# Earlier weight preparation, a last pair stored in two halves, and result operations moved behind the root in a conv, norm and table-FFN kernel

## The chip, the cores and the metric

The kernel runs on one core of a Trainium2 chip. The metric is the device time of one execution in microseconds, the median of several runs. The engines are named as the profile names them: PE is TensorE (PEld is its weight load), DVE is VectorE, ACT is ScalarE, POOL is GpSimd, SP is SyncE, whose queue here issues all transfers of x and of the result.

## The reference

The input x is 8 images of 256 channels by 64 by 64 pixels, f32.

```python
x = x + conv3x3_mean(ln_over_channels(x, eps=1e-6))   # 1/9 box, depthwise, zero padding
t = tokens(x)                                          # one token per pixel, 256 values
n = ln(t, eps=1e-5)
# four argmax nibbles of (n[16:80] > 0.5), two operator values and flags n[0:3] > 0.5
# build a sparse 80-wide row for two positions; three 80x80 layers with relu between (two weight sets);
# features 50 and 79 of the result give two rounded values 0..15 and a carry
out = n + 2*one_hot(lo) in 64..79 + 2*one_hot(hi) in 72..87 + carry in channel 80
x = image(t + out)
```

So per pixel: normalise over channels, blur, add, normalise again, and add to channels 64 to 87 what a small network says.

## The kernel before, in words

A pair of images lies in SBUF with its 2 x 64 rows on the 128 partitions, and for each partition 256 channels by 64 columns. There are 4 pairs, and a pair is worked in 8 chunks of 8 columns (CW), so there are 32 chunks. All engines run one software pipeline of 38 steps, written out in order for each engine (`run_steps`). In step t chunk t gets its first statistics, chunk t-1 is normalised (split into f16 high and low parts nhi and nlo), chunk t-2 is convolved, chunk t-3 is decoded and gets its final normalisation, chunks t-4 and t-5 are in the network, and chunk t-6 gets its result operations.

DVE's list in a step is the subject of most of the edit. `add_convolution(s)` (L570) adds the convolved pair of columns s from PSUM and waits for PE. `x_statistics` and `x1_statistics` (L552) are the variances. `finish(0..4)` are small operations: reciprocal of the root that ACT made, a Newton step, and in `finish(4)` the gains, shifts and the threshold `thr` (L456), whose semaphore `fin_ready` starts POOL (L659, L669) and the decoding. `put(0..7)` are the result operations of chunk t-6: `put(0)` waits for the transposed results of PE (`yt_done`, after L918) and runs L467 and L469, `put(4)` is the one-hot comparison L481, `put(5)` and `put(6)` (L488) and `put(7)` (L491) add into x and count `hotc`. `pick(0..2)` decode (L503, L505, L510, L513), and `normalise` (L542) makes the input of ACT's nhi (L816), which POOL's nlo (L650) and then PE's convolution (L864) need. POOL ends a step with the feature rows (L723), which PE transposes (L927) before it goes on to `convolve(1)`.

ACT applies the final normalisation to seven of the eight columns of a chunk (`columns`, L771), two, two and one of them in step t-3's groups s = 1, 2, 3 and the last two in the next step, and then counts `out_ready`. POOL does the eighth (L697, `out_p`).

The weights come through ACT's own queue (L756, 27 small transfers). `setup_parts` on DVE (L383 to L405) splits the first layer into three bf16 parts and runs at the start of step 2; PE's transposes of the weights (L840, L842) stand in its step 2 ahead of the first convolution; `setup_weights` on DVE (L409 to L415) copies them from PSUM in step 3.

SP stores channels in ranges. The range LATE is the one that the result operations write and waits for `hotc`; the ranges EARLY wait only for `out_ready` and `out_p`. Half a pair (32 columns) is stored at a time, so that one contiguous run in HBM is 128 bytes. The last pair is stored in four parts of 16 columns (LAST_PARTS), with runs of 64 bytes, one after the other in the queue: EARLY of a part, then its LATE, then the next part.

Of the kernel before, what the change touches and what calls it, by code (L numbers as in the profile page):

```python
# [9 lines left out]
ALU = mybir.AluOpType  # L10
# [13 lines left out]
GROUPS = CW // 2  # L24
HALVES = 2
HALF_W = W // HALVES
EARLY = ((0, C // 4), (C // 2, C))
LATE = (C // 4, C // 2)
RANGES = EARLY + (LATE,)


LAST_PARTS = (0, W // 4, W // 2, 3 * W // 4, W)


ALU_LO, ALU_HI, AX_LO, OP_COL, OUT_LO, OUT_HI, CARRY = 16, 32, 48, 65, 64, 72, 80
# [103 lines left out]
def build(nc, x_d, wa_d, ba_d, ws_d, bs_d, cst_d, out_d):  # L139
    with ExitStack() as ctx:  # L140
# [3 lines left out]
        def sem(name):  # L144
            return ctx.enter_context(nc.semaphore(name))
# [112 lines left out]
        y_read = sem("y_read")  # L258
        out_ready = sem("out_ready")
        out_p = sem("out_p")  # L260
        hotc = sem("hotc")

        def xview(parity):
# [9 lines left out]
        @block.sync  # L273
        def _(sp):
            def tile_part(parity, img, chans, cols):

                c0, c1 = chans
                return xbuf[img * H:(img + 1) * H, bass.ds(parity * (C * W) + c0 * W, (c1 - c0) * W)] \
                    .rearrange("p (c w) -> p c w", w=W)[:, :, cols[0]:cols[1]]

            def dram_part(ap, pair, img, chans, cols):
                return ap[bass.ds(pair * IMGS + img, 1), chans[0]:chans[1], :, cols[0]:cols[1]] \
                    .rearrange("b c h w -> (b h) c w")

            def load(pair, parity, chans, cols, loaded):
                for img in range(IMGS):
                    sp.dma_start(tile_part(parity, img, chans, cols), dram_part(x_d, pair, img, chans, cols)) \  # L287
                        .then_inc(loaded, 16)

            def store(pair, chans, cols, signal):  # L290
                for img in range(IMGS):
                    sp.dma_start(dram_part(out_d, pair, img, chans, cols),
                                 tile_part(pair % 2, img, chans, cols)).then_inc(signal, 16)

            sp.dma_start(cst[:, :], cst_d).then_inc(cst_loaded, 16)
            for pair in range(2):
                for h in range(HALVES):
                    if pair > 0:
                        sp.wait_ge(x_loaded[h], HALF_TILE * pair)
                    for chans in RANGES:  # L300
                        load(pair, pair, chans, (h * HALF_W, (h + 1) * HALF_W), x_loaded[h])

            def leave(pair, i, h):

                cols = (h * HALF_W, (h + 1) * HALF_W)
                store(pair, RANGES[i], cols, stored[h][i])

            def enter(pair, i, h):
                sp.wait_ge(stored[h][i], 16 * IMGS * (pair + 1))
                load(pair + 2, pair % 2, RANGES[i], (h * HALF_W, (h + 1) * HALF_W), x_loaded[h])  # L310

            def chunks_by(pair, h):

                return pair * CHUNKS + (h + 1) * (CHUNKS // HALVES)

            late = len(EARLY)
            with sp.Fori(0, PAIRS - 2) as pair:
                for h in range(HALVES):
                    sp.wait_ge(x_loaded[h], HALF_TILE * (pair + 2))
                for h in range(HALVES):  # L320
                    sp.wait_ge(out_ready, chunks_by(pair, h))
                    sp.wait_ge(out_p, chunks_by(pair, h))
                    for i in range(late):
                        leave(pair, i, h)
                    for i in range(late):
                        enter(pair, i, h)
                    sp.wait_ge(hotc, chunks_by(pair, h) * HOT_STEPS)
                    leave(pair, late, h)
                    enter(pair, late, h)
            pair = PAIRS - 2  # L330
            for h in range(HALVES):
                sp.wait_ge(out_ready, chunks_by(pair, h))
                sp.wait_ge(out_p, chunks_by(pair, h))
                for i in range(late):
                    leave(pair, i, h)
                sp.wait_ge(hotc, chunks_by(pair, h) * HOT_STEPS)
                leave(pair, late, h)
            pair = PAIRS - 1
            for cols in zip(LAST_PARTS, LAST_PARTS[1:]):
                chunks = pair * CHUNKS + cols[1] // CW  # L340
                sp.wait_ge(out_ready, chunks)
                sp.wait_ge(out_p, chunks)
                for chans in EARLY:
                    store(pair, chans, cols, last_stored)
                sp.wait_ge(hotc, chunks * HOT_STEPS)
                store(pair, LATE, cols, last_stored)
            for h in range(HALVES):
                for i in range(len(RANGES)):
                    sp.wait_ge(stored[h][i], 16 * IMGS * (PAIRS - 1))
            sp.wait_ge(last_stored, 16 * IMGS * len(RANGES) * (len(LAST_PARTS) - 1))  # L350

        @block.vector
        def _(v):
# [104 lines left out]
            def result(i, last, k):  # L458
# [14 lines left out]
                if i == 1:  # L473
                    v.tensor_reduce(ycar2, ycar, mybir.AxisListType.X, ALU.add).then_inc(y_read, 1)
                    hc.count(v.tensor_scalar(yr, yr, 1.0, float(NIB), ALU.max, ALU.min))
                elif i == 2:
                    hc.count(v.tensor_tensor(yr, yr, over(msk[:, k, :, :].unsqueeze(2), four), ALU.mult))
                elif i == 3:
                    hc.count(v.tensor_reduce(yrr, yr, mybir.AxisListType.X, ALU.add))
                elif i == 4:  # L480
                    hc.count(v.tensor_tensor(hot,  # L481
                                             over(cst[:, K_IOTA:K_IOTA + NIB].unsqueeze(1).unsqueeze(2), hot_shape),
                                             over(yrr.unsqueeze(3), hot_shape), ALU.is_equal))
                elif i in (5, 6):
                    at = OUT_LO if i == 5 else OUT_HI
                    v.wait_ge(out_ready, c + 1)
                    v.wait_ge(out_p, c + 1)
                    hc.count(v.scalar_tensor_tensor(cols[:, :, at:at + NIB], hot[:, :, i - 5, :], 2.0,  # L488
                                                    cols[:, :, at:at + NIB], ALU.mult, ALU.add))
                else:  # L490
                    hc.count(v.tensor_tensor(cols[:, :, CARRY], cols[:, :, CARRY], ycar2, ALU.add))  # L491
                    hc.end()
# [24 lines left out]
            def step(t, j, pair):  # L517
# [61 lines left out]
                    if tok:  # L579
                        decode(i, tok, (j - 1) % 4)  # L580

                if known(t) and t == 2:
                    setup_parts()
                if known(t) and t == 3:
                    setup_weights()
                if first:
                    half = {0: 0, CHUNKS // HALVES: 1}.get(j)
# [2 lines left out]
                add_convolution(0)  # L590
                x_statistics(0)
                wait_x1(0)
                put(0)
                x1_statistics(0)
                put(1)
                x_statistics(1)
                finish(0)
                put(2)
                finish(1)
                put(3)  # L600
                finish(2)
                put(4)
                finish(3)
                add_convolution(1)
                finish(4)
                if tok:
                    v.wait_ge(fin_ready, t)
                pick(0)
# [8 lines left out]
                normalise(CW - 2)  # L617
                wait_x1(2)
                pick(2)
                x1_statistics(2)  # L620
                x_statistics(2)
                put(5)
# [111 lines left out]
        def _(act):  # L734
# [25 lines left out]
            def step(t, j, pair):  # L760
# [5 lines left out]
                def columns(chunk, k, begin, end):  # L766

                    c, jc, par = chunk
                    for w in range(begin, end):
                        col = xview(par)[:, jc * CW + w, :]  # L770
                        ins = act.activation(col, col, ACT.Identity, bias=shift[:, k, w:w + 1],  # L771
                                             scale=gain[:, k, w:w + 1])
                    if end == CW - 1:
                        ins.then_inc(out_ready, 1)

                for s in range(GROUPS):
# [23 lines left out]
                        act.activation(s_sqrt[:, (j - 1) % 2, :], s_var[:, (j - 1) % 2, :],  # L800
                                       ACT.Sqrt).then_inc(sqrt_ready, 1)
                    if s == 0 and ffn:
                        columns(ffn, (j - 2) % 4, OUT_AT[GROUPS - 1], CW - 1)
                    if s == 0 and ffn:
                        c, jc, par = ffn
                        act.wait_ge(ft_done, c + 1)
# [16 lines left out]
                    if tok and s > 0:  # L823
                        if s == 1:
                            act.wait_ge(u_read, tok[0] + 1)
                            act.wait_ge(g_read, DV_STEPS * tok[0] + 1)
                        columns(tok, (j - 1) % 4, *OUT_AT[s - 1:s + 1])

            run_steps(act, step)

# [1 line left out]
        def _(pe):  # L832
# [35 lines left out]
            def step(t, j, pair):  # L868
# [1 line left out]
                ffn = chunk_at(t, j, pair, 4)  # L870
                back = chunk_at(t, j, pair, 5)
                last = chunk_at(t, j, pair, 6)
                if known(t) and t == 2:
                    setup_weights()
                if known(t) and t == 4:
                    pe.wait_ge(setup_v, SETUP_V)
                for s in range(GROUPS):
                    if conv:
# [96 lines left out]
```

## Time and profile before

| | |
|---|---|
| median of 3 runs | 617.44 us (616.48 to 617.96) |
| profiled execution | 618.25 us |
| its span in the profile | 616.5 us |
| DVE busy | 507.8 us (82%) |
| PE busy | 479.6 us (78%) |
| ACT busy | 468.7 us (76%) |
| POOL busy | 383.9 us (62%) |
| SP's transfer queue | 591696 packets, 67.30 MB |

The profiled execution took 1.75 us more than its span, for what lies around it. Busy shares are means over the whole span: the first 25 us are the load of the first half pair, then some steps fill the pipeline, then come some 26 full steps, and after about 545 us the pipeline drains.

### The profile page before, as it was taken

What the parts mean: (1) busy time and instruction counts of PE and PEld (TensorE: products, weight loads), DVE (VectorE), ACT (ScalarE), POOL (GpSimd) and SP (SyncE); (2) the same over time, 40 slices, a digit from 0 to 9 for tenths busy, and PEclk for the clock granted to TensorE, in tenths of its full rate; (3) what the DMA queues carried; (4) which work ended last, traced back from release to release, by engine and by line L of the source; (5) the groups of instructions that cost most, each with busy time, mean ns of one, the idle gap of its engine ahead of it and who ended that gap; (6) DMA issues with size and microseconds to landing.
All of it is one profiled execution on the core that took longest, in us unless ns stands there. A gap on an engine that the chain in (4) does not pass through costs nothing.

```text
span 616.5 us, 8862 instructions
## 1 busy us (share of the span) xinstructions
PE 479.6 (78%) x2294; PEld 201.1 (33%) x2294; DVE 507.8 (82%) x1476; ACT 468.7 (76%) x675; POOL 383.9 (62%) x676
## 2 busy tenths in 40 slices
PE   0035369999989988988899999988999999997750
PEld 0012123333333434333333333433333333433220
DVE  1378979999999999999999999999999999874130
ACT  0011569888888888899999888888888888998730
POOL 0044767777777777777777777777777777764000
PEclk9997779999999999999999999999999999998885
DMA  9999990099877995699559958960598099898998
GB/s 168 191 193 199 193 164 2 0 109 170 133 104 104 171 172 68 103 166 190 80 78 176 173 89 110 137 70 1 68 115 92 1 103 69 64 75 62 88 87 72
DMA packets 592746, 67.97 MB, mean 110 GB/s; under 512 B 592568, under 2 KB 592696, under 8 KB 592696
## 3 DMA queue, kind: packets, MB, share of 16 engines
q1 hardware_dynamic: 591696, 67.30, 88.5%
q8 instruction: 19, 0.31, 0.2%
q14 instruction: 31, 0.25, 0.1%
q10 hardware_dynamic: 1000, 0.11, 0.1%
HBM read 33.84 MB, written 33.55 MB: 109 GB/s over the span
## 4 chain that ended last, share of the span: by engine, by line
DVE 33%; PE 32%; POOL 12%; ACT 11%; issue 5%; SPq 3%; DMA 1%; DVEq 0%; POOLq 0%; ACTq 0%
PE ps L864 13%; PE ps L895 10%; POOL nlo L650 10%; DVE n L542 9%; DVE stat L552 7%; ACT nhi L816 5%; PE ps L918 4%; DVE g L505 4%; DVE xbuf L570 3%; ACT xbuf L771 3%; SPq L287 3%; PE ps L887 2%; DVE ps L481 2%; ACT h L791 1%; PE ps L900 1%
## 5 line engine op out<-in xcount | busy, mean ns | idle before, releaser
L771 ACT ACTIVATE xbuf<-xbuf,shift,gain 128x256 f32<-128x256 f32 x224 | 200.4, 944 | 0.0
L552 DVE BATCH_NORM_STATS2 stat<-xbuf 128x6 f32<-128x512 f32 x256 | 171.2, 685 | 22.0 <-DMA xbuf<-x 21.8
L650 POOL TENSOR_TENSOR nlo<-n,nhi 128x1024 f16<-128x1024 f32 x64 | 137.5, 2149 | 7.5 <-ACT nhi L816 7.4
L895 PE MATMUL ps<-h,w2m 128*128 128x512 f32 x256 | 134.3, 607 | 3.7 <-ACT h L791 2.4
L864 PE MATMUL ps<-nhi,band 128*128 128x512 f16 (+1 forms) x408 | 108.4, 380 | 25.1 <-POOL nlo L650 25.1
L669 POOL TENSOR_SCALAR n<-xbuf,stat,rns 128x256 f32<-128x256 f32 x64 | 94.2, 1478 | 41.4 <-DVE ps L456 41.0
L542 DVE SCALAR_TENSOR_TENSOR n<-xbuf,stat,ps 128x256 f32<-128x256 f32 x192 | 118.8, 663 | 0.1
L864 PE MATMUL ps<-nlo,band 128*128 128x512 f16 (+1 forms) x408 | 107.4, 377 | 0.0
L570 DVE TENSOR_TENSOR xbuf<-ps,xbuf 128x512 f32<-128x512 f32 x128 | 91.5, 715 | 15.6 <-PE ps L864 15.5
L816 ACT ACTIVATE nhi<-n 128x1024 f16<-128x1024 f32 x64 | 67.5, 1054 | 46.6 <-DVE n L542 46.6
L791 ACT ACTIVATE h<-ps,b2m 128x512 f32<-128x512 f32 x128 | 88.0, 687 | 11.4 <-PE ps L895 11.3
L783 ACT ACTIVATE h<-ps 128x512 f32<-128x512 f32 x128 | 75.7, 591 | 19.5 <-PE ps L887 19.5
L659 POOL TENSOR_TENSOR ut<-xbuf,stat 128x16 f32<-128x16 f32 x32 | 7.4, 230 | 123.8 <-DVE ps L456 123.8
L864 PEld LDWEIGHTS ps<-nhi,band 128*128 128x128 f16 x408 | 35.6, 100 | 110.9 <-issue 55.2
L887 PE MATMUL ps<-featT,w 128*128 128x512 bf16 x128 | 49.7, 388 | 28.4 <-ACT featT L808 26.4
L864 PEld LDWEIGHTS ps<-nlo,band 128*128 128x128 f16 x408 | 41.0, 100 | 45.5 <-issue 5.5
L895 PEld LDWEIGHTS ps<-h,w2m 128*128 128x128 f32 x256 | 45.6, 191 | 25.0 <-issue 17.6
L467 DVE SCALAR_TENSOR_TENSOR ps<-ps,msk 128x16 f32<-128x16 f32 x32 | 5.8, 183 | 47.9 <-PE ps L918 47.9
L723 POOL TENSOR_TENSOR feat<-val,msk 128x264 bf16<-128x264 bf16 x64 | 39.1, 635 | 0.2
L918 PEld LDWEIGHTS ps<-consts,ysb 128*128 128x128 f32 x256 | 33.5, 192 | 16.4 <-ACT ysb L821 9.0
L912 PE MATMUL ps<-h2r,w3r 128*128 128x512 f32 x64 | 36.0, 645 | 0.0
L900 PE MATMUL ps<-h,w2r 128*32 128x512 f32 x256 | 35.8, 633 | 0.0
(90 smaller groups left out, 560.0 us busy)
## 6 DMA issues: line engine op xcount, KB each, us to landing
xbuf<-x SPq DMA_DIRECT2D x32, 512.0 KB, 6.9
xbuf<-x SPq DMA_DIRECT2D x16, 1024.0 KB, 11.1
out<-xbuf SPq DMA_DIRECT2D x32, 512.0 KB, 7.4
out<-xbuf SPq DMA_DIRECT2D x12, 1024.0 KB, 12.6
out<-xbuf SPq DMA_DIRECT2D x16, 256.0 KB, 8.3
consts<-cst SPq DMA_DIRECT2D x1, 176.0 KB, 2.4
h<-ws ACTq DMA_DIRECT2D x4, 0.2 KB
b2r<-bs ACTq DMA_DIRECT2D x4, 0.1 KB
```

What stands on the lines that cost most here:

```text
L542: ins = v.scalar_tensor_tensor(n32[:, w // HALF, w % HALF, :], xview(par)[:, jc * CW + w, :], mean[:, k, w:w + 1], over(rn[:, w:w + 1], [P ...
L552: return v.bn_stats(stat[:, j % 4, at + 2 * s:at + 2 * s + 2, :].rearrange("p w n -> p (w n)"), xview(par)[:, w:w + 2, :].rearrange("p w c ...
L570: v.tensor_tensor(pair_cols, ps[:, B_CONV + s % 2, :].rearrange("p (w c) -> p c w", w=2), pair_cols, ALU.add).then_inc(x1_done, 1)
L650: pool.tensor_tensor(nlo[:, at:at + HALF, :], n32[:, h, :, :], nhi[:, at:at + HALF, :], ALU.subtract).then_inc(lo_ready, 1)
L669: pool.tensor_scalar(n32[:, h, HALF - 1, :], xview(par)[:, jc * CW + w, :], mean[:, k, w:w + 1], rns[:, j % 2, w:w + 1], ALU.subtract, ALU ...
L771: ins = act.activation(col, col, ACT.Identity, bias=shift[:, k, w:w + 1], scale=gain[:, k, w:w + 1])
L783: act.activation(h1[:, slot(i, jc), :], ps[:, B_L1, :], ACT.Relu).then_inc(h1_ready, 1)
L791: act.activation(h2[:, slot(i, jc), :], ps[:, B_L2, :], ACT.Relu, bias=b2m[:, 0:1]).then_inc(h2_ready, 1)
L816: act.activation(nhi[:, at:at + HALF, :], n32[:, s - 1, :, :], ACT.Copy).then_inc(hi_ready, 1)
L864: ins = pe.matmul(bank[:, i:i + k, :], band[:, :], src[:, at:at + k, :], start=n == 1, stop=n == 2 * len(pieces))
L887: pe.matmul(ps[:, B_L1, :], w1[:, i % 2, :], featT[:, jc % 2, i // 2, :], start=True, stop=True).then_inc(l1_done, 1)
L895: pe.matmul(ps[:, B_L2, :], w2m[:, :], h1[:, slot(i, jc), :], start=True, stop=True).then_inc(l2_done, 1)
```

## The change

The weights are prepared in step 0 on DVE and PE: parts, transposes and copies all stand before DVE's first wait for x. LATE shrinks from channels 64..127 to 64..95 and EARLY's second range grows to 96..255; this is so for all loads and stores. The last pair is stored in two parts of 32 columns. For the very last chunk ACT normalises columns 0 to 3 in one go, DVE columns 4 to 6 (a new `tensor_scalar`, with its own semaphore `out_v`), POOL the eighth as ever. In every step the statistics come before `finish(0)`, `put(0)` to `put(3)` each stand behind the `finish` of the same number, and `put(4)` behind `finish(4)`.

```diff
-EARLY = ((0, C // 4), (C // 2, C))
-LATE = (C // 4, C // 2)
+EARLY = ((0, C // 4), (3 * C // 8, C))
+LATE = (C // 4, 3 * C // 8)
-LAST_PARTS = (0, W // 4, W // 2, 3 * W // 4, W)
+LAST_PARTS = (0, W // 2, W)
 ...
                 sp.wait_ge(out_ready, chunks)
+                if chunks == NCHUNK:
+                    sp.wait_ge(out_v, 1)
 ...
-                if known(t) and t == 2:
+                if t == 0:
                     setup_parts()
-                if known(t) and t == 3:
                     setup_weights()
 ...
                 wait_x1(0)
-                put(0)
                 x1_statistics(0)
-                put(1)
                 x_statistics(1)
                 finish(0)
+                put(0)
+                finish(1)
+                put(1)
+                finish(2)
                 put(2)
-                finish(1)
+                finish(3)
                 put(3)
-                finish(2)
-                put(4)
-                finish(3)
                 add_convolution(1)
                 finish(4)
+                put(4)
                 if tok:
                     v.wait_ge(fin_ready, t)
                 pick(0)
 ...
                 pick(2)
+                if tok and tok[0] == NCHUNK - 1:
+                    c, jc, par = tok
+                    k = (j - 1) % 4
+                    v.wait_ge(u_read, c + 1)
+                    for w in range(HALF, CW - 1):
+                        col = xview(par)[:, jc * CW + w, :]
+                        ins = v.tensor_scalar(col, col, gain[:, k, w:w + 1], shift[:, k, w:w + 1], ALU.mult, ALU.add)
+                    ins.then_inc(out_v, 1)
 ...
                     if s == 0 and ffn:
-                        columns(ffn, (j - 2) % 4, OUT_AT[GROUPS - 1], CW - 1)
+                        if ffn[0] < NCHUNK - 1:
+                            columns(ffn, (j - 2) % 4, OUT_AT[GROUPS - 1], CW - 1)
 ...
-                        columns(tok, (j - 1) % 4, *OUT_AT[s - 1:s + 1])
+                        if tok[0] < NCHUNK - 1:
+                            columns(tok, (j - 1) % 4, *OUT_AT[s - 1:s + 1])
+                        elif s == 1:
+                            columns(tok, (j - 1) % 4, 0, HALF)
 ...
-                if known(t) and t == 2:
+                if t == 0:
                     setup_weights()
```

## Rows read from the trace of the kernel before

**Rows 1.** The page: span, and the busy share of the 16 DMA engines in 40 slices

```profile
span 616.5 us, 8862 instructions
DMA  9999990099877995699559958960598099898998
```

**Rows 2.** Timeline of the start: start us, us, engine, line, operation, [idle before, releaser]

```profile
25.55 2.47 DVE L552 BATCH_NORM_STATS2 stat<-xbuf 128x6 f32<-128x512 f32 x4 [21.82 <-DMA xbuf<-x]
...
34.04 4.21 POOL L650 TENSOR_TENSOR nlo<-n,nhi 128x1024 f16<-128x1024 f32 x2
...
36.11 2.23 DVE L386 COPY h<-h 128x2 f32<-128x2 f32 x2
...
40.54 0.09 DVE L404 MEMSET h<- 128x12 bf16 x2
...
41.80 1.27 PE L864 MATMUL ps<-nhi,band 128*128 128x512 f16 x3
...
44.24 0.72 DVE L570 TENSOR_TENSOR xbuf<-ps,xbuf 128x512 f32<-128x512 f32 x1 [3.61 <-PE ps L864]
...
57.78 1.49 PE L864 MATMUL ps<-nlo,band 128*128 128x512 f16 x3
...
59.68 0.73 DVE L570 TENSOR_TENSOR xbuf<-ps,xbuf 128x512 f32<-128x512 f32 x1
```

**Rows 3.** DMA queue of the weights: packets from 0 to 15 us, and all

```profile
q10 hardware_dynamic: 1000, 0.11, 5.4%
q10 hardware_dynamic: 1000, 0.11, 0.1%
```

**Rows 4.** Timeline of one full step, DVE, ACT and PE in order of time

```profile
291.50 0.17 DVE L456 TENSOR_TENSOR ps<-stat,ps 128x8 f32<-128x8 f32 x1
...
304.01 0.18 DVE L467 SCALAR_TENSOR_TENSOR ps<-ps,msk 128x16 f32<-128x16 f32 x1 [0.77 <-PE ps L918]
...
304.18 0.23 ACT L800 ACTIVATE s_sqrt<-s_var 128x16 f32<-128x16 f32 x1
...
304.39 0.62 PE L927 MATMUL ps<-identb,feat 128*128 128x128 bf16 x8 [0.52 <-POOL feat L723]
...
305.49 0.81 PE L864 MATMUL ps<-nlo,band 128*128 128x512 f16 x3
...
306.16 0.43 DVE L481 TENSOR_TENSOR ps<-consts,ps 128x256 f32<-128x256 f32 x1
...
306.58 0.71 DVE L570 TENSOR_TENSOR xbuf<-ps,xbuf 128x512 f32<-128x512 f32 x1
...
307.64 0.16 DVE L456 TENSOR_TENSOR ps<-stat,ps 128x8 f32<-128x8 f32 x1
307.83 0.18 DVE L503 TENSOR_TENSOR marks<-xbuf,ps 128x24 f32<-128x24 f32 x1
```

**Rows 5.** Timeline of the 33rd step, in which DVE waits for the second convolution

```profile
531.52 0.81 PE L864 MATMUL ps<-nlo,band 128*128 128x512 f16 x3
532.37 0.71 DVE L570 TENSOR_TENSOR xbuf<-ps,xbuf 128x512 f32<-128x512 f32 x1 [0.29 <-PE ps L864]
```

**Rows 6.** Timeline of the drain: ACT's columns of the last chunk, DVE's last operation

```profile
567.51 1.78 ACT L771 ACTIVATE xbuf<-xbuf,shift,gain 128x256 f32<-128x256 f32 x2
...
576.91 1.12 ACT L808 ACTIVATE featT<-ps 128x1024 bf16<-128x1024 bf16 x1
...
597.46 0.16 DVE L491 TENSOR_TENSOR xbuf<-xbuf,ps 128x8 f32<-128x8 f32 x1
```

**Rows 7.** Windows of the last store part: us, busy of PE, PEld, DVE, ACT, POOL, clock, DMA share, GB/s

```profile
577.80:601.00 23.20, 15.34 (x66) 5.40 (x66) 4.68 (x20) 8.47 (x14) 0.00 (x0) 0.81 1.17 88
```

**Rows 8.** DMA from 451.4 to 471 us, and the first store issued in it: KB, us to landing

```profile
q1 hardware_dynamic: 24617, 3.14, 140.9%
out<-xbuf SPq DMA_DIRECT2D x1, 512.0 KB, 4.9
```

**Rows 9.** Waits of SP's queue at the end: us in total, times, longest

```profile
SPq L350 <- DMA out<-xbuf: 5.1, 1, 5.1
```

More of the change, by code:

```diff
@@ L260, in build @@
         out_p = sem("out_p")
+        out_v = sem("out_v")
         hotc = sem("hotc")
@@ L486, in result @@
                     v.wait_ge(out_ready, c + 1)
+                    if c == NCHUNK - 1:
+                        v.wait_ge(out_v, 1)
                     v.wait_ge(out_p, c + 1)
@@ L772, in columns @@
                                              scale=gain[:, k, w:w + 1])
-                    if end == CW - 1:
+                    if end == CW - 1 or c == NCHUNK - 1:
                         ins.then_inc(out_ready, 1)
@@ L872, in step @@
                 last = chunk_at(t, j, pair, 6)
-                if known(t) and t == 2:
+                if t == 0:
                     setup_weights()
-                if known(t) and t == 4:
+                if t == 4:
                     pe.wait_ge(setup_v, SETUP_V)
```

## The prediction, as put on record

> **What bounds the kernel now.** I read the page first, then the timeline of its three stretches, since no mean describes them all. In the start nothing runs until 25.55 us, when DVE's first statistics stop waiting for x; DVE then waits again for PE, 3.61 us ahead of the eviction at 44.24 [rows 2]. In the full steps the chain goes round through all engines: from one threshold operation (L456, 291.50) to the next (307.64) it is 16.14 us, and DVE's only idle time in it is 0.77 us at `put(0)`, waiting for PE's transposed results [rows 4]. In the drain DVE's last operation ends at 597.62 [rows 6], but the span ends at 616.5 [rows 1]: the last 19 us are stores alone. They are late because the queue was still busy: the DMA slices are full there [rows 1], and the part before moved at only 88 GB/s in its 64-byte runs [rows 7]. So there are three places, each with its own limit.
>
> **Weights in step 0.** Before, the first convolution starts at 41.80, behind the weight work. Its input, the first of POOL's two low parts, is ready at half of 4.21 us after 34.04, so 36.15 [rows 2]. With about 0.14 us to hand it over, PE starts at 36.29; start to eviction is 44.24 - 41.80 = 2.44, so the eviction goes at 38.73 in place of 44.24: 5.5 us. The two statistics and the root that follow come after it in order, so the whole pipeline shifts. In step 3 the low-part matmuls of the first convolution end at 57.78 + 1.49 = 59.27, and the eviction goes at 59.68 because the weight copies lie between; with the 0.04 us that an eviction needs after its matmuls (531.52 + 0.81 = 532.33 against 532.37 [rows 5]) that is 0.37 more. Sum 5.9.
>
> What the move costs in its new place must fit before 25.55. All 1000 packets of ACT's queue have started by 15 us [rows 3]; landed they are by some 17, an estimate from the last starts and from a 512 KB store, which takes 4.9 us from issue to landing [rows 8] of which these small ones need only the end. The parts took 36.11 to 40.63 = 4.5 us, PE's transposes the time up to 41.80, 1.2 us [rows 2], and the five copies at most 1.2 (between 0.18 and 0.43 each, the small PSUM rows [rows 4]). 17 + 6.9 = 23.9, so it costs nothing under the load of x; the cover left is 1.6 us, and what exceeds it is paid one to one. Everything queued behind the wait for the weights on DVE (all statistics) would be late then; on PE and ACT nothing is. One of the copies, 36.11, takes 2.23 us with its neighbour and ends within 0.1 us of POOL's low part (34.04 + 4.21 = 38.25) [rows 2]. The Trainium skill (SBUF — State Buffer, Who interferes with whom) says that a DVE copy in a two-port mode and a GpSimd operation exclude each other for a whole instruction. The trace agrees with it, and by it, with POOL idle in step 0, the cover would be 3.7 instead of 1.6 us; the sum is the same.
>
> **Result operations later.** It looks as if 0.77 us a step, times some 26, would go. I don't take that. Take the wait away, and the next limit is the loop through POOL: L456 -> decode and three normalised columns -> nhi -> nlo -> POOL's list -> features -> L927 -> second convolution -> eviction -> `finish(4)` -> L456. PE's L927 waited for POOL's features, 0.52 us; the second convolution ends at 305.49 + 0.81 = 306.30, and DVE evicted it at 306.58 [rows 4], where 306.34 was possible. So that loop has 0.24 us to give: 15.90. Now `put(4)` stands between L456 and the decoding, in that very loop. It is 0.43 us long, and the next eviction follows it with one small operation between (306.16 to 306.58), so some 0.34 of it count [rows 4]; but between L456 at 307.64 and L503 at 307.83 DVE idles for the semaphore, 0.1 us of which it fills; I take 0.24 as what it adds. The loop comes to 15.90 + 0.24 = 16.14, as before: DVE's wait moves from `put(0)` to `add_convolution(1)`. Bounds: nothing added, -0.24 x 26 = -6.2 us; the whole 0.43 added, +0.19 x 26 = +4.9. The last two full steps waited at the eviction already, 0.29 [rows 5], and can only lose `put(4)`'s 0.24 each, +0.5; with a little gained in the first such step I book +0.2 for all of it. `finish(0)` now comes some 1.2 us earlier and needs ACT's root, which ends at 304.41 [rows 4]; DVE would arrive there within 0.1 us of that, and the chain from it to the eviction has more room than that.
>
> **The last chunk's columns.** Seven columns on ACT become four, in one go from 567.51. At 1.78 for two [rows 6] they end at about 571.0 instead of 577 (the copy that follows them started at 576.91 [rows 6]). DVE's three are a form that the trace doesn't show; between a 0.18 small operation and the 0.71 of an eviction twice as large [rows 4], so at most 2.1 us for three, or some 3 with a wait for POOL, which still ends before ACT's four. ACT's list after it is shorter by three columns, 2.7 us; ACT and PE hand each other tiles there and PE's own time fills part, so of 0 to 2.7 I take 0.9 off the end of the network.
>
> **Stores.** LATE's shrinking moves channels 96..127 to the stores that don't wait for results. In the middle no engine waits for these transfers, so it is free there. At the end: EARLY of the second half is 224 channels x 128 rows x 128 bytes = 3.67 MB. It starts at `out_ready`, 571.0 - 5.9 + 0.2 = 565.3 in new time. Rows 8 show what such a store costs: 3.14 MB in 128-byte runs between 451.4 and 471, so 19.3 us with its start; 7/6 of that is 22.5, to 587.8. The last result operation ends at 597.62 - 5.9 + 0.2 - 0.9 = 591.0. So the queue is empty then, and only LATE of a half is left, 0.52 MB: 4.9 us from issue for the same bytes [rows 8], 5.3 as it is two transfers. The wait on the last landing was 5.1 before [rows 9], much the same. To close I take 0.6, an estimate. 591.0 + 5.3 + 0.6 = 596.9.
>
> The Trainium skill (DMA: Bandwidth & Descriptors, Why small descriptors are slow) gives each packet a fixed 3 cycles beside one for each 32 bytes. By that a 128-byte run costs 7 where a 64-byte run costs 5, and the half would leave at 88 x 10/7 = 126 GB/s, the span ending at 601.7 as in rival 3; rows 8 show more, 3.14 MB / 19.3 us = 163 GB/s, and the sum goes by that.
>
> **Sum.** 616.5 - 596.9 = 19.6 us less. The profiled execution (618.25 with 1.75 around its span) lies 0.8 above the median 617.44, so the median should come to 596.9 + 1.75 - 0.8 = 597.8.
>
> **Rivals.** (1) The step loop gets shorter after all, because the wait that goes is not replaced: up to -6.2 us, 591.6. For it: DVE's only idle time goes; against: L927's wait for POOL. Chance 0.1. (2) `put(4)` in the loop costs its whole length, +4.9: 602.7. The gap of 0.19 before L503 speaks against. Chance 0.1. (3) The end stays bound by the queue: if the second half moves half way between 88 and 163 GB/s, at 126, EARLY takes 29.1 us from 566.3, to 595.4, and LATE 4.2, then 2.1 for landing and closing (4.9 less the 3.2 that 0.52 MB take at 163, with 0.4 to 0.6 to close): span 601.7, median 602.6. At the whole 88 of rows 7 it is 41.7 + 6.0 and the span 616, no change. Chance 0.13, of which 0.02 for no change. (4) The weights land late or their chain is slow, the cover of 1.6 is exceeded and most of the 5.9 goes: 603.5. Chance 0.06. (5) Slower than before: ACT's root. In step after step `finish(0)` to `finish(4)` and all of `put` now stand behind the wait for it, with only the statistics ahead. If the root came late enough for DVE to lose more than 0.75 us a step on top of 16.14, 26 steps would eat the 19.6; at 1 us a step it is 624. The root would have to be some 1.6 us later than its 304.41, and ACT runs in the same order as ever. Chance 0.03.
>
> **Numbers.** My forecast 597.8 has 0.58, with its own range of 594.5 to 600.5. The range of 592.5 to 603.5 takes in most of rivals 1 to 4. A measurement of this kernel tells some 0.2%, 1.2 us, from no change. Faster 0.95, within it 0.02, slower 0.03.
>
> **What would show it.** Right: first convolution on PE at about 36.3; L456 to L456 still about 16.1, with DVE idle ahead of L570 of the second convolution and none ahead of L467; ACT's L771 x4 once near 562; the last DVE operation near 591, and about 6 us behind it. Wrong: DVE's first statistics after 26; steps of 15.9 or 16.4; stores of the last half still moving when the results are done.

## The result, and the profile after

The changed kernel takes 596.5 us (median of 4 runs, 593.87 to 596.77), the kernel before 617.7 in the same session (616.48 to 618.1): ratio 0.965, 95% interval 0.962 to 0.968, so 3.5% faster, 1.3 us under the forecast of 597.8. The profiled execution is the fastest of the four, 593.87 with a span of 592.1; the other spans are 594.7 to 595.0. What I read from the profile is therefore some 2.6 us better than the median, and the section on the reasons says where.

The page of the kernel after (span; the busy share of the DMA engines in 40 slices; the chain that ended last, by engine):

```profile
span 592.1 us, 8823 instructions
...
DMA  9999990099945998299939994590209511990299
...
POOL 41%; DVE 23%; PE 17%; ACT 9%; issue 4%; SPq 3%; DMA 1%; POOLq 0%; ACTq 0%; DVEq 0%
```

A slice is 14.8 us. Where [rows 1] reads 8 or 9 from the 33rd slice to the end, four slices here, the 33rd, 34th, 37th and 38th, are almost empty (1, 1, 0 and 2). The last two still read 9; that the queue runs dry in the last one and then moves one short burst shows only in the windows further down. POOL has become the largest part of the chain (12% before).

The start, from the timeline (the columns are those of [rows 2]):

```profile
15.03 0.31 DVE L389 COPY h<-h 128x2 f32<-128x2 f32 x3 [11.25 <-DMA b<-bs]
...
17.54 0.09 DVE L407 MEMSET h<- 128x12 bf16 x2
...
17.94 1.06 PE L858 MATMUL ps<-consts,h 128*128 128x128 f32 x4
...
19.71 0.28 DVE L418 COPY w3r<-ps 128x128 f32<-128x128 f32 x1
...
25.75 2.47 DVE L557 BATCH_NORM_STATS2 stat<-xbuf 128x6 f32<-128x512 f32 x4 [5.77 <-DMA xbuf<-x]
...
34.26 4.19 POOL L662 TENSOR_TENSOR nlo<-n,nhi 128x1024 f16<-128x1024 f32 x2
...
36.43 1.25 PE L880 MATMUL ps<-nhi,band 128*128 128x512 f16 x3 [17.43 <-POOL nlo L662]
...
38.78 0.71 DVE L575 TENSOR_TENSOR xbuf<-ps,xbuf 128x512 f32<-128x512 f32 x1 [2.64 <-PE ps L880]
```

The weights are there at 15.03, all work on them is done at 19.99, and DVE then still waits 5.77 us for x. The first convolution starts at 36.43 (it was 41.80) and the first eviction at 38.78 (44.24).

One full step from the timeline, in order of time, and ahead of it the threshold operation (L459, before L456) of the 7th and, at the end, of the 31st step:

```profile
121.69 0.17 DVE L459 TENSOR_TENSOR ps<-stat,ps 128x8 f32<-128x8 f32 x1
...
295.48 0.62 PE L943 MATMUL ps<-identb,feat 128*128 128x128 bf16 x8 [0.50 <-POOL feat L735]
295.54 0.26 DVE L441 RECIPROCAL ps<-s_sqrt 128x16 f32<-128x16 f32 x1
295.71 0.12 DVE L470 SCALAR_TENSOR_TENSOR ps<-ps,msk 128x16 f32<-128x16 f32 x1
...
296.58 0.81 PE L880 MATMUL ps<-nlo,band 128*128 128x512 f16 x3
...
297.43 0.71 DVE L575 TENSOR_TENSOR xbuf<-ps,xbuf 128x512 f32<-128x512 f32 x1 [0.72 <-PE ps L880]
...
298.50 0.16 DVE L459 TENSOR_TENSOR ps<-stat,ps 128x8 f32<-128x8 f32 x1
...
298.57 0.42 DVE L484 TENSOR_TENSOR ps<-consts,ps 128x256 f32<-128x256 f32 x1
...
298.90 0.17 DVE L508 TENSOR_TENSOR marks<-xbuf,ps 128x24 f32<-128x24 f32 x1
...
507.59 0.17 DVE L459 TENSOR_TENSOR ps<-stat,ps 128x8 f32<-128x8 f32 x1
```

`put(0)` (L470) has no wait in front of it now; the wait stands at the eviction (L575), 0.72 us, and ends 0.04 us behind the second convolution (296.58 + 0.81 = 297.39). This is the wait that the prediction named. A step takes (507.59 - 121.69) / 24 = 16.08 us, against 16.14 in [rows 4] (16.16 as a mean of the same 24 steps of before).

The drain: DVE's new columns, ACT's four, and DVE's last operation from the timeline:

```profile
555.56 2.28 DVE L630 TENSOR_SCALAR xbuf<-xbuf,gain,shift 128x256 f32<-128x256 f32 x3
...
558.68 3.41 ACT L783 ACTIVATE xbuf<-xbuf,shift,gain 128x256 f32<-128x256 f32 x4
...
586.62 0.16 DVE L496 TENSOR_TENSOR xbuf<-xbuf,ps 128x8 f32<-128x8 f32 x1
```

The same stretch in windows (columns as in [rows 7]):

```profile
565.00:570.00 5.00, 3.63 (x25) 2.26 (x29) 2.34 (x10) 3.48 (x6) 0.00 (x0) 1.00 1.52 175
...
583.00:585.00 2.00, 0.97 (x8) 0.87 (x8) 0.71 (x5) 0.00 (x0) 0.00 (x0) 0.95 1.02 107
585.00:587.00 2.00, 0.00 (x0) 0.00 (x0) 1.60 (x6) 0.00 (x0) 0.00 (x0) 0.50 0.03 6
...
588.00:590.00 2.00, 0.00 (x0) 0.00 (x0) 0.00 (x0) 0.00 (x0) 0.00 (x0) 0.50 1.12 183
```

ACT's columns end at 562.09. EARLY of the second half then leaves at 175 GB/s, twice the 88 of [rows 7], and is over at about 584.3 (107 of 175 in the window from 583). Results are done at 586.78, 2.5 us later, and only LATE is left. From there to the end of the span it is 5.3 us.

### The profile page after: what moved, and what is told of

It reads as the page before. It is cut to its first block, busy times and chain, and to the rows that moved or that the text cites. A ratio compares the mean times of both kernels' runs of the same rounds, so it can differ in the third digit from the quotient of the medians.

```text
span 592.1 us, 8823 instructions
## 1 busy us (share of the span) xinstructions
PE 477.5 (81%) x2294; PEld 200.3 (34%) x2294; DVE 506.7 (86%) x1479; ACT 466.7 (79%) x672; POOL 384.6 (65%) x676
## 4 chain that ended last, share of the span: by engine, by line
POOL 41%; DVE 23%; PE 17%; ACT 9%; issue 4%; SPq 3%; DMA 1%; POOLq 0%; ACTq 0%; DVEq 0%
POOL nlo L662 21%; PE ps L880 9%; DVE n L547 8%; POOL feat L735 5%; ACT nhi L829 5%; DVE xbuf L575 4%; POOL xbuf L709 4%; DVE g L510 4%; SPq L288 3%; PE ps L943 3%; PE ps L911 2%; ACT xbuf L783 2%; DVE stat L557 2%; POOL nhit L718 1%; POOL val L706 1%
## 5 line engine op out<-in xcount | busy, mean ns | idle before, releaser
L783 ACT ACTIVATE xbuf<-xbuf,shift,gain 128x256 f32<-128x256 f32 x221 | 197.6, 944 | 0.0
L557 DVE BATCH_NORM_STATS2 stat<-xbuf 128x6 f32<-128x512 f32 x256 | 166.4, 683 | 5.8 <-DMA xbuf<-x 5.8
L575 DVE TENSOR_TENSOR xbuf<-ps,xbuf 128x512 f32<-128x512 f32 x128 | 91.7, 716 | 33.0 <-PE ps L880 33.0
L829 ACT ACTIVATE nhi<-n 128x1024 f16<-128x1024 f32 x64 | 67.5, 1054 | 38.2 <-DVE n L547 38.2
L916 PE MATMUL ps<-h,w2r 128*32 128x512 f32 x256 | 34.6, 613 | 0.0
L925 PE MATMUL ps<-h,w 128*32 128x512 f32 x256 | 34.1, 604 | 0.0
```

The lines of the kernel that those rows point to most:

```text
L557: return v.bn_stats(stat[:, j % 4, at + 2 * s:at + 2 * s + 2, :].rearrange("p w n -> p (w n)"), xview(par)[:, w:w + 2, :].rearrange("p w c ...
L575: v.tensor_tensor(pair_cols, ps[:, B_CONV + s % 2, :].rearrange("p (w c) -> p c w", w=2), pair_cols, ALU.add).then_inc(x1_done, 1)
L829: act.activation(nhi[:, at:at + HALF, :], n32[:, s - 1, :, :], ACT.Copy).then_inc(hi_ready, 1)
```

## The experiments

Each kernel was timed against the kernel before in the same session, whose median moved a little between sessions (617.05 to 618.43). So I compare ratios; 0.001 is 0.6 us.

### The three parts alone

**e1_weights** is the kernel before with only the weights in step 0:

```diff
-                if known(t) and t == 2:
+                if t == 0:
                     setup_parts()
-                if known(t) and t == 3:
                     setup_weights()
```

> The kernel before with the weight preparation in step 0 and nothing else. My theory, from the two traces: the whole pipeline moves up by what the first four steps show, 81.23 - 73.45 = 7.8 us at the threshold operation of step 4, of which the prediction had booked 5.9; so about 610 us (617.7 - 7.8). Rival: the additional 1.9 us of steps 3 and 4 come from the other parts of the change; then 611.8. Second rival: the first half load's end is the only thing that counts and the later steps wait for x; then less than 2 us.

612.24 us (610.83 to 614.75), ratio 0.9906 (0.9876 to 0.9935): 5.8 us less. The interval is 4.0 to 7.7 us, so the 5.9 of the prediction fits, and the 7.8 that was expected here, from the changed kernel's profile between its start and its sixth step, lies just outside. In e1's own profile the sixth threshold operation comes at 106.75, 6.69 us ahead of the kernel before, and both profiles have one long step at the start (17.29). The changed kernel's profile has none: some of the first steps may be 1.4 us longer or not from run to run, as the last experiments show.

**e2_stores** is the kernel before with only the ranges and the parts:

```diff
-EARLY = ((0, C // 4), (C // 2, C))
-LATE = (C // 4, C // 2)
+EARLY = ((0, C // 4), (3 * C // 8, C))
+LATE = (C // 4, 3 * C // 8)
-LAST_PARTS = (0, W // 4, W // 2, 3 * W // 4, W)
+LAST_PARTS = (0, W // 2, W)
```

> The kernel before with the new ranges and the last pair in two parts, nothing else. Theory: the second half's EARLY can start only when ACT's last two columns of the last chunk are done, at about 577.1, takes 22.5 us to 599.6, and LATE follows it, some 5 us with its landing: span about 605, median 606.3, a gain of 11.4. Rival: the queue is not the limit and the end follows the last result operation at 597.6 by 5.9 us: 604.7. Rival on the other side: starting the second half 10 us later than the third quarter did costs as much as the longer runs give: 617.

606.03 us (604.65 to 608.97), ratio 0.9791 (0.9756 to 0.9826): 12.1 us less (606.3 was expected), the largest part by far. 7.0 us lie between the last result operation (600.20) and the end of the span (607.2), against 5.3 in the changed kernel.

**e3_order** is the kernel before with only DVE's new order of `put` and `finish`:

```diff
                 wait_x1(0)
-                put(0)
                 x1_statistics(0)
-                put(1)
                 x_statistics(1)
                 finish(0)
+                put(0)
 ...
                 finish(4)
+                put(4)
```

> The kernel before with the new order of DVE's result operations, nothing else. Theory: the wait of 0.77 us a step at the first result operation reappears at the eviction of the second convolution, since the loop through POOL now holds the one-hot comparison; the step goes from 16.16 to about 16.07 us as in the trace of the changed kernel, so 26 x 0.09 = 2.4 us less: 615.3. Rival 1: the order is worth the whole wait, 20 us less. Rival 2: nothing, 617.7.

616.61 us (614.7 to 618.01, 12 runs), ratio 0.9973 (0.9955 to 0.9991): 1.5 us less (2.4 were expected), small but outside what the measurement leaves open. Its waits over the whole span (in total, times, longest):

```profile
DVE xbuf L570 <- PE ps L864: 34.7, 40, 3.4
...
DVE ps L467 <- PE ps L918: 23.7, 3, 11.3
```

In the kernel before, L467 waited 32 times, now 3 times (the drain), and the eviction 14 times, now 40. So the wait moved and did not go. The step is 16.08 us.

The three ratios multiply to 0.9906 x 0.9791 x 0.9973 = 0.967, and the whole change has 0.965, 1.4 us more. The split of the last chunk's columns is in the whole and in none of the three, and e5 below puts it at 2.7 us; the intervals of the three together are some 3 us wide to either side, so the parts add up as far as these runs can tell.

### What put(4) costs, and what bounds the step behind it

**e4_put4_early** is the changed kernel with `put(4)` out of the loop:

```diff
                 put(3)
+                put(4)
                 add_convolution(1)
                 finish(4)
-                put(4)
```

> The changed kernel with put(4) moved from behind finish(4) to ahead of add_convolution(1), where DVE waits 0.72 us for PE. Theory (the loop through POOL is the limit and put(4) stands in it with 0.21 us): the step goes from 16.07 to about 15.86, 27 x 0.21 = 5.7 us less, 596.5 - 5.7 = 590.8; DVE's wait at the eviction shrinks by about 0.5. Rival 1 (the step is limited by DVE's own list or by ACT's): no change, 596.5. Rival 2: the comparison now holds up the eviction, slower.

593.15 us (589.16 to 593.82), ratio 0.9576 (0.9545 to 0.9607). Its regular step is 15.91 us, so `put(4)` adds 16.08 - 15.91 = 0.17 a step. The median is 3.3 us (4.6 by the ratios) below the changed kernel's. 5.7 were expected, from 0.21 a step; 27 steps of 0.17 are 4.6. The profiled run, the slowest of the six, also has three long steps: 4, 5 and 10 take 17.33, 17.37 and 17.55 us. The step with 17.55, PE's timeline, behind the same instructions one step earlier:

```profile
153.41 0.62 PE L943 MATMUL ps<-identb,feat 128*128 128x128 bf16 x8 [0.50 <-POOL feat L735]
153.86 0.81 PE L880 MATMUL ps<-nhi,band 128*128 128x512 f16 x3
154.51 0.81 PE L880 MATMUL ps<-nlo,band 128*128 128x512 f16 x3
...
169.31 0.98 PE L943 MATMUL ps<-identb,feat 128*128 128x128 bf16 x8 [0.52 <-POOL feat L735]
170.09 1.49 PE L880 MATMUL ps<-nhi,band 128*128 128x512 f16 x3
171.37 1.49 PE L880 MATMUL ps<-nlo,band 128*128 128x512 f16 x3
```

And that kernel's windows, where the third number from the end is the granted clock:

```profile
166.00:170.00 4.00, 3.03 (x20) 2.14 (x20) 4.00 (x15) 4.00 (x8) 3.25 (x3) 0.93 0.47 80
170.00:174.00 4.00, 3.90 (x15) 1.56 (x18) 2.05 (x14) 2.44 (x4) 0.00 (x0) 0.65 0.47 72
```

The six convolution matmuls took 2.77 us from the first start to the last end where they take 1.46. The granted clock is 0.65 in the mean of the window, that is, partly at the lower of its two levels (1.2 GHz), after a stretch in which PE waited for POOL's features.

**e8_norm_first** goes on from e4: the first three normalised columns ahead of `pick(0)`, since nhi waits for them (ACT's L829: 0.42 us in the changed kernel, 0.26 in e4):

```diff
+                for w in range(HALF - 1):
+                    normalise(w)
                 if tok:
                     v.wait_ge(fin_ready, t)
                 pick(0)
-                for w in range(HALF - 1):
-                    normalise(w)
```

> The kernel e4_put4_early with pick(0) moved behind the first three normalised columns. Theory: ACT's nhi can start 0.9 us earlier after the threshold, POOL's own list then decides when the first nlo starts (0.2 us earlier), and the loop through POOL goes from 15.91 to about 15.7 a step, where ACT's list of 15.65 is the next limit: 27 x 0.2 = 5.4 us under e4, about 588. Rival 1: the step is limited by something else at 15.9, no change from e4, 593. Rival 2: PE's idle times grow and its clock falls more often, at 1.6 us each time; slower than 593.

585.11 us (583.0 to 587.24), ratio 0.945 (0.9423 to 0.9476). The step is 15.75 us (about 15.7 expected), and the kernel is 2.9 us faster than expected. Of the 8.0 us to e4 the steps give 27 x 0.16 = 4.3; in the profiles another 1.6 is e4's long tenth step, and the rest isn't explained. A piece of its chain of waits (start us, us, what):

```profile
297.27 0.23 POOL ut L671
297.50 3.03 POOL n L681 x2
300.53 0.20 POOL u L689
...
300.83 2.19 POOL nlo L662
```

Here POOL goes from the threshold to its low part without waiting for ACT. But POOL's loop isn't the only limit. DVE and PE at the end of the same step, from the timeline:

```profile
310.79 0.81 PE L880 MATMUL ps<-nlo,band 128*128 128x512 f16 x3
...
311.10 0.43 DVE L484 TENSOR_TENSOR ps<-consts,ps 128x256 f32<-128x256 f32 x1
...
311.63 0.71 DVE L575 TENSOR_TENSOR xbuf<-ps,xbuf 128x512 f32<-128x512 f32 x1
```

DVE's `put(4)` ends at 311.53, the convolution at 311.60, and the eviction starts at 311.63 with no wait in front of it. From 120 to 520 us DVE waits 1.2 us in all, where it waits 8.1 in e4 and 18.1 in the changed kernel. So DVE's own list and the loop through POOL are now about equally long, and a still shorter step needs less work in both; no run tests that.

### The columns and the stores of the end

**e5_no_split** is the changed kernel with all seven last columns on ACT, as before:

```diff
-                if tok and tok[0] == NCHUNK - 1:
 ...
-                        ins = v.tensor_scalar(col, col, gain[:, k, w:w + 1], shift[:, k, w:w + 1], ALU.mult, ALU.add)
-                    ins.then_inc(out_v, 1)
```

> The changed kernel, but ACT normalises all seven columns of the last chunk as in every other chunk. Theory: the second half's EARLY starts some 5.3 us later (about 567.5 instead of 562.2 in the trace's time) and its packets end at about 590 instead of 585, past the last result operation (586.8 + about 1 for ACT's longer list); LATE then queues behind them: about 2.5 to 3 us slower than the changed kernel, 599.5. Rival: the split only shortens ACT's list, 1 us: 597.6. Second rival: the queue was the limit already, then the whole 5.3: 602.

599.77 us (598.61 to 602.63), ratio 0.9694 (0.9656 to 0.9732): about 2.7 us more than the changed kernel (599.5 was expected). ACT's last column ends at 571.51, 9.4 us later than in the changed kernel. 2.7 us of that, as of the 5.1 us at the last operation (591.90 against 586.78), are two long steps at its start: 17.28 and 17.33, where the changed kernel's profile has 15.89 and 16.06. From the 34th threshold to the last operation it is 35.16 us here and 33.60 there, 1.6 more. Its windows behind the last operation:

```profile
592.00:594.00 2.00, 0.00 (x0) 0.00 (x0) 0.00 (x0) 0.00 (x0) 0.00 (x0) 0.67 1.39 148
594.00:596.00 2.00, 0.00 (x0) 0.00 (x0) 0.00 (x0) 0.00 (x0) 0.00 (x0) 0.50 0.99 153
596.00:598.00 2.00, 0.00 (x0) 0.00 (x0) 0.00 (x0) 0.00 (x0) 0.00 (x0) 0.50 0.74 114
```

The queue is still moving EARLY when the results are done, and the end is 599.1 - 591.9 = 7.2 us behind them, not 5.3. So 1.9 us of what the split of the columns brings is that the queue runs dry in time.

**e6_four_parts** is the changed kernel with four parts for the last pair again:

```diff
-LAST_PARTS = (0, W // 2, W)
+LAST_PARTS = (0, W // 4, W // 2, 3 * W // 4, W)
```

> The changed kernel with the last pair stored in four parts of 16 columns again (64-byte runs). Theory: from the 28th chunk's results at about 549 us on, 4.5 MB must leave at the 88 to 97 GB/s of such runs, 46 to 51 us, so the span ends near 600 to 603 and the median near 604.5, 8 us over the changed kernel. Rival: with the smaller LATE range and the earlier columns the four parts overlap as well with the drain as the two halves do: 597.

608.96 us (605.86 to 609.29), ratio 0.9841 (0.981 to 0.9872): 11.8 us more than the changed kernel, where 8 were expected. Its last result operation ends at 587.01, as in the changed kernel (586.78), but the span at 604.1: the queue carries 86 GB/s from 567 to 580 and 85 from 580 to 600, against 175.

**e7_late64** is the changed kernel with the channel ranges as before:

```diff
-EARLY = ((0, C // 4), (3 * C // 8, C))
-LATE = (C // 4, 3 * C // 8)
+EARLY = ((0, C // 4), (C // 2, C))
+LATE = (C // 4, C // 2)
```

> The changed kernel with LATE at channels 64 to 127 as before. Theory: what is left after the last result operation doubles from 0.52 to 1.05 MB, 4096 packets more at 1.35 to 1.7 a nanosecond, 2.4 to 3 us: 599.6. Rival: only the landing of the last packet counts, no change.

598.33 us (597.29 to 599.41), ratio 0.9673 (0.9641 to 0.9705): some 1.4 us more by the ratios, whose intervals overlap (599.6 was expected). In its profile the last operation ends at 587.2 and the span at 595.5, 8.3 us later where it was 5.3. So by the profile the smaller LATE is worth 3 us at the end, by the ratios half of it.

### Long steps and PE's clock

Are the long steps made by PE's clock? e5's kernel is the changed kernel up to the last chunk, so their profiles can be compared step by step. In the fourth step, ahead of the second convolution, the changed kernel (15.89 us) has

```profile
70.29 0.62 PE L943 MATMUL ps<-identb,feat 128*128 128x128 bf16 x8 [1.20 <-POOL feat L735]
70.74 0.81 PE L880 MATMUL ps<-nhi,band 128*128 128x512 f16 x3
```

and e5 (17.28 us)

```profile
70.70 1.03 PE L927 MATMUL ps<-identb,feat 128*128 128x128 bf16 x8 [2.37 <-POOL feat L723]
71.53 1.49 PE L864 MATMUL ps<-nhi,band 128*128 128x512 f16 x3
```

(L927 and L864 are the same instructions under e5's line numbers.) Over these transposes and the convolution the granted clock was 1.00 in the changed kernel (70.3 to 72.2 us) and 0.54 in e5 (70.7 to 74.1). If the clock makes the long steps, work for PE in its idle 0.50 us should prevent them. **e9_after_fill** is the changed kernel, **e10_put4_fill** e4 and **e11_norm_fill** e8, each with eight transposes that nobody reads, ahead of PE's wait for the features:

```diff
-                        pe.wait_ge(feat_ready, c + 1)
                         wait(pe, y_copied, c - 1)
+                        for b in range(CW):
+                            pe.transpose(ftp[:, b * P:(b + 1) * P], identb[:, :], identb[:, :])
+                        pe.wait_ge(feat_ready, c + 1)
```

> The changed kernel with eight transposes that nobody reads, put on PE ahead of its wait for the feature rows (line L943 and its wait), where PE idles 0.50 us in a step. They take 0.46 us each time, so they fit in the idle time and add at most 0.1 us to a step. If the long steps (17.2 to 17.6 us in place of 16.08) come from PE's granted clock, which fell ahead of L943 in them, PE has hardly any idle time left there, such steps become rarer or vanish, the slow step at the start goes too, and the median comes to the fastest run of the changed kernel or close: about 594, against 596.5. If they come from something else (a transfer, POOL), the fillers change nothing and the median stays at 596.5, or is some 1 to 2 us longer where they delay the transposes.

> The same eight fillers in the kernel with put(4) ahead of add_convolution(1), whose regular step is 15.91 us and in whose profile one step of the loop took 17.55 and two of the start 17.33 and 17.37, all three with L943 and the convolution at the lower clock level. Clock theory: steps of 15.91 throughout, no long ones, median near 590.5 against 593.15. Otherwise 593 or more, and long steps remain.

> The same eight fillers in the kernel that has the first three normalised columns ahead of pick(0), whose step is 15.75 us and whose median was 585.11. Its first steps were 16.99 and 17.24 long. Clock theory: those two come down to about 15.8 to 16, median near 583. Otherwise 585 or more.

| | without fillers | with | ratio without | ratio with | steps 4 and 5 without | with |
|---|---|---|---|---|---|---|
| changed kernel (e9) | 596.5 | 594.72 | 0.965 | 0.9627 | 15.89, 16.06 | 15.84, 15.86 |
| e4 (e10) | 593.15 | 590.09 | 0.9576 | 0.9554 | 17.33, 17.37 | 15.76, 16.77 |
| e8 (e11) | 585.11 | 583.35 | 0.945 | 0.9451 | 16.99, 17.24 | 15.56, 16.44 |

The tenth step, e4's long one, in e10's timeline:

```profile
165.90 0.61 PE L941 MATMUL ps<-identb 128*128 128x128 bf16 x8
166.55 0.62 PE L945 MATMUL ps<-identb,feat 128*128 128x128 bf16 x8
167.00 0.81 PE L880 MATMUL ps<-nhi,band 128*128 128x512 f16 x3
167.65 0.81 PE L880 MATMUL ps<-nlo,band 128*128 128x512 f16 x3
```

With fillers no profile has a step over 16.8 us, where e4 has three and e8 two over 16.9. That is one profile of each kernel, and it isn't proof: the profiles of the changed kernel, of e6 and of e7 have no such step without fillers either. e9's five runs lie within 0.9 us (594.18 to 595.04) where the changed kernel's four spread over 2.9, but e10's still spread over 1.9 and e11's over 3.1. The medians are lower by 1.8, 3.1 and 1.8, but the kernel before was also 0.7 to 1.4 us faster in that session: by the ratios it is 1.4, 1.4 and nothing, and the intervals overlap. So that a long step is one in which PE's transposes and the convolution behind them run at the lower clock is shown by the timelines; that the fillers prevent it is likely and not shown, and what they gain in the median isn't settled.

## Why the prediction was right, point by point

**Start, 5.9 us.** Right. PE's first convolution was forecast for about 36.3 and came at 36.43, the eviction for 38.73 and came at 38.78. The part alone measured 5.8. The threshold operation of the second step came 5.45 us earlier, that of the third 6.38: 5.9 were booked, so 0.5 more went in step 3 than the 0.37. By the sixth step the profiled run was 7.81 ahead. The 1.4 us between are the step of 17.29 us that the kernel before has at its start and this profile hasn't (15.89); that is this run, not the change.

**The cover.** Booked as 1.6 us, measured 5.77: the weights were there at 15.03 and not some 17, and the work took 5.0 us and not 6.9. The first copies took 0.31 us for three where one with its neighbour took 2.23 [rows 2], and POOL was idle. By the Trainium skill's rule (SBUF — State Buffer, Who interferes with whom), under which such a copy and a POOL operation exclude each other, a short copy was to be expected in step 0, and this trace agrees with it. Rival 4 needed the cover to be used up, and it was far from it.

**The order on DVE.** The mechanism is right: the wait went from `put(0)` to the eviction, and the loop through POOL is next to bound the step. The forecast for that loop without `put(4)` was 15.90, and e4 shows 15.91. The size of one term was off: `put(4)` was booked at 0.24 a step and measured 0.17 (16.08 - 15.91); the gap between the threshold and L508 grew from 0.19 [rows 4] to 0.40, 0.21. The step was to be 16.14 and is 16.08, and over the loop that is -1.5 (e3) or -1.9 (the profile: 7.81 ahead at the sixth step, 9.70 at the 34th) where I booked +0.2. Rivals 1 and 2 were the two ends of this term; the truth was a third of the way from my value towards the first. Rival 5 did not come up: DVE's reciprocal (L441) waits three times in the whole span, 4.7 us in all.

**Columns.** 0.9 booked off the end of the network. Between the 34th threshold (9.70 ahead) and the last operation (10.84 ahead) it was 1.1; against e5, which differs in the columns alone, 1.6. DVE's new form took 0.76 us each, so the upper of the bounds 0.18 and 0.71 was a little too low; the three took 2.28, inside the 2.1 to 3 given for them. What I did not book is the second effect, that the stores start earlier: without it the queue would have been the limit, 1.9 us (e5).

**Stores.** EARLY of the second half was to take 22.5 us and took 22.2 (562.1 to 584.3). The tail was to be 5.9 and is 5.3. The rate of 163 GB/s from [rows 8] was a mean that contained a start; the steady rate is 175. By the rule for small descriptors in the Trainium skill (DMA: Bandwidth & Descriptors, Why small descriptors are slow) the prediction's estimate was 126. The measurement decides: the rule doesn't fit this queue's 88 at 64 bytes and 175 at 128, where the rate doubles with the run. Rival 3 failed on that, but its place was well chosen. (Its sum starts EARLY at 566.3, the main sum at 565.3; no row has the 1.0 between.) The queue is empty only 2.5 us ahead of the results, and e5 shows it as the limit once the columns come late.

**The sum.** In the profiled run the last operation was forecast for 591.0 and ended at 586.78. The 4.2 us are 0.5 of the third step, 1.4 of the long step that this run hasn't, 2.1 of the loop and 0.2 of the columns; 0.6 of the tail make the span 4.8 shorter than forecast. The other three runs' spans are 2.6 to 2.9 us longer. e5's profile shows what can make that: both steps long, 34.61 us where the changed kernel's profile has 31.95, 2.66 more. If the other three had them too, which no profile shows, the median follows: the terms of the change were forecast 0.5 + 2.1 + 0.2 + 0.6 = 3.4 us too long, and two things went the other way, one long step more than in the profile of before (some 1.3), and the 0.8 by which I put the median under the profile. 1.3 us are left. So the terms are right in kind, but that the forecast hit within 1.3 us is in part luck: its largest error, 2.1 us in the loop, was offset by steps that it didn't know of.

## What to carry to other kernels

Where an order on an engine removes a wait, look for the loop that is next and cost in it every operation that the new order puts there: here the wait of 0.77 us a step gave 0.08, and moving one comparison out of the loop and three columns forward gave 0.33 more. At the end of a kernel ask at what time the queue runs dry and at what time the last result is there; wider runs and earlier inputs for the stores pay until these two meet. A profile is one run: compare its time with the median before a difference of one or two us in it is given to the change.

## What the runs showed of the hardware that I had not expected

A short loss of PE's clock lengthens the whole step in a loop that goes round all engines. In e4's tenth step the granted clock fell behind PE's wait for the features, the transposes took 0.98 instead of 0.62 us and the six convolution matmuls 2.77 instead of 1.46, and the step 17.55 instead of 15.91. The steps behind it were regular again, and nothing made up for the 1.6 us. The same step of the changed kernel, with the same idle time, shows none of it. At the start of the pipeline such steps are common: in the window from 82 to 86 us the granted clock was 0.59 in e1 and 0.50 in e4 (long steps), and 0.87 in the changed kernel (none). They are not confined to it: e1 and e2 have one in the middle as well (two steps there take 33.61 and 33.65 us together, where two regular ones take 32.3), and in both the transposes took 1.03 us; the granted clock was 0.75 in e1's window from 428 to 432.

Stores in runs of 128 bytes moved at 174 to 175 GB/s, in runs of 64 bytes at 85 to 88, so one run cost this queue about the same time at either size.
